# Attention stages on one Trainium2 core: turns and maxima in 64-row halves, value products in two blocks, PSUM banks in three pairs

## The chip, the cores and the metric

One core of one Trainium2 chip runs the whole program in one launch. The metric is the device time in microseconds (us). Three runs of the kernel before took 2137.2, 2140.37 and 2140.66 us; the median is 2140.37 us.

TensorE is called PE here, VectorE DVE, ScalarE ACT, GpSimd POOL, and SyncE, which issues most DMAs, SP.

## The reference, cut to what matters

Two decoder layers over x of shape (16, 256, 256), sixteen heads of 16 columns, all in fp32. Each layer is: attention over x itself, attention over a context of 77 rows, a feed-forward part. Every one of them reads its input through a layer norm and adds its output to x.

```
q, k, v = x @ Wq + bq, c @ Wk + bk, c @ Wv + bv      # c is x or the context
scores  = einsum('bhqd,bhkd->bhqk', q, k) / sqrt(16) # masked: window of 32 / causal / padding / a mask
out     = softmax(scores) @ v                        # per head
x       = x + out @ Wo + bo
```

The four attentions are of kind `window`, `cross_pad` (layer 0), `causal` and `cross_mask` (layer 1). Layer 0's feed-forward part is a mixture of eight experts, two for each row; layer 1's is a quantised gated one. The change touches neither.

## The kernel before, in words

`attention` (line 188) is called twice: for window and cross_pad, then for causal and cross_mask. Each call is one software pipeline of `N` = 32 items (a batch entry in a layer), one step an item. A step `t` works on item t (layer norm turned, q, k, v projected), item t-1 (scores, row maxima), item t-2 (scores again, shifted by the maxima, then exp and the value product) and item t-3 (last value product, heads turned and divided, output projection); item t-4's output is added to x. Every step has 8 slots, `i` = 0 to 7 (`PAIRS_H`), one for each pair of heads. Each engine runs its own written-out order of a step and meets the others only at semaphores, so the order inside `step` of each engine sets everything.

What a slot holds on PE (`step`, line 1672): `scores` (line 1536) writes the raw scores of a pair into the bank pair `ps1`, once DVE has taken the last pair's maxima (`s1_max`). `shifted` (line 1564) writes minus the row maximum (a product with `selects`) and the scores again into the bank pair `ps2`, once ACT's exp of the last pair is done (`expd`). Both take 64 rows of PE, the two halves side by side. Both bank pairs have one buffer. In the two cross layers a slot of even `i` does two pairs and a slot of odd `i` none (`L.pairs` = 2; `wide(ref)` says so of item t-2). Behind `shifted` comes what is left of the step, one thing or two a slot:

- slot 0: `turn_normed` (four 128-row transposes of the normalised x), the fourth value product `pv` of item t-3
- slot 1: the query projection, `max_out` of the second half of item t-2's maxima
- slot 2: the key projection (self-attention only), parts of the routing or of the last layer norm's turn
- slot 3: `pv` of quad 0 (a quad is four heads; 32 columns of PE each); slot 4: the value projection, `max_out` of item t-1's first half; slots 5 to 7: `pv` of quads 1 and 2, and for item t-3 the turn of the heads (line 1791), the turn of the divided output (1805) and the output projection (1819)

PSUM has four bank pairs: ps1, ps2, `pso` (value products of four quads) and `misc`, which in turn holds the turned x, q, k, v, the maxima, the heads and the output product; PE's waits on `oT_ev`, `m_ev`, `added`, `v_ev` guard it. `prob` holds two quads. DVE (line 1188) does in each slot `row_max` (line 1015), and between them: `split_max` ahead of slot 0 and in slot 3, `add_output` in 0, the next item's statistics in 1, `low_part` of q in 2 and of k in 3, the heads' reciprocal and division ahead of row_max in slot 6, `merge_rows` (causal only) in 4 to 7, `normalise` of the next item in 7. ACT (line 1404) does the exps and copies PSUM out: xT, o_aug (all four quads at once), q and k high parts, v, maxima, oT. POOL cuts the masks out of `prob` (`cut`), SP moves q and k parts into `q_pair` and `k_pair` (`stacked`).

Of the kernel before, what the change touches and what calls it, by code (L numbers as in the profile page):

```python
# [4 lines left out]
F32 = mybir.dt.float32  # L5
# [136 lines left out]
class Route:  # L142

    def __init__(self, nc, ctx, a, room):
# [18 lines left out]
        self.got_in = ctx.enter_context(nc.semaphore("moe_got_in"))  # L163
        self.half_in = ctx.enter_context(nc.semaphore("moe_half_in"))
        self.first_rows = self.got[:, 0, 0:1, :]
        self.first_rows_in = ctx.enter_context(nc.semaphore("moe_first_rows_in"))
# [5 lines left out]
        self.first_in = ctx.enter_context(nc.semaphore("moe_first_in"))  # L172
        self.first_w = [ctx.enter_context(nc.semaphore(f"moe_first_w{i}")) for i in range(3)]
# [14 lines left out]
def attention(nc, layers_in, x_sb, q_pair, k_pair, v_aug, ident, selects, to_all, eye, parts, merge=None, tail=None, route=None,  # L188
# [8 lines left out]
    with ExitStack() as ctx:  # L197
# [8 lines left out]
        prob = sb("prob", [P, 2, 2, 2, S + P], F32)  # L206
# [6 lines left out]
        masked = sb("masked", [P, 4 * S], BF16)  # L213
# [11 lines left out]
        bv_wide = sb("bv_wide", [P, KC, P], F32)  # L225
# [7 lines left out]
        if tail or route:  # L233
            last_ln = layernorm_tiles(lambda name, shape, dt: sb(f"last_{name}", shape, dt))
            last_xn = [sb("last_xn", [P, ST, D], F32)[:]] if tail else route.rows
# [60 lines left out]
        pso = pb("pso", [P, 2, 512])  # L296
        misc = pb("misc", [P, 2, 512])
# [105 lines left out]
        bank = lambda k: misc[:, k, :]  # L403
        xT_ps = bank(0).rearrange("p (k t) -> p k t", k=KC)
        q_ps = bank(1).rearrange("p (k t) -> p k t", k=KC)
        o_heads = misc[:, :, :].rearrange("p a (h d) -> p (a h) d", d=VW)
        o_by_half = o_tok[:].rearrange("p s (q a j) d -> p a (s q) j d", a=2, j=2)
        oT_ps = misc[:, :, 0:S].rearrange("p a (n t) -> p a n t", t=64)
# [3 lines left out]
        ctx_ps = lambda n: (ps2[:, 0, :], ps2[:, 1, :], pso[:, 1, :])[n % 3].rearrange("p (k t) -> p k t", k=KC)  # L412
# [7 lines left out]
        def k_ps(par, L):  # L420
            if L.cross:
                return L.k_now[par][:]
            return bank(0)[:, 0:KC * L.nk].rearrange("p (k t) -> p k t", k=KC)

        def v_ps(L):
            return bank(1)[:, 0:L.ktiles * D].rearrange("p (k h d) -> p (k h) d", k=L.ktiles, d=HD)
# [33 lines left out]
        def turned_before(ref):  # L460

            return active(ref, 2) and active(ref, 3) and layer_at(ref, 2).pairs == 1

        def cut_early(ref):

            return turned_before(ref) and layer_at(ref, 2).kind == "causal"

# [28 lines left out]
        def turn_bank(ref, k):  # L496
# [2215 lines left out]
```

## Time and profile before

| | |
|---|---|
| median of three runs | 2140.37 us |
| span of the profiled execution | 2144.3 us |
| PE / DVE / ACT / POOL busy, share of the span | 93% / 58% / 45% / 32% |
| window stage, first to last query projection | 10.9 to 305.3 us |
| cross_pad stage, the same | 323.7 to 572.1 us |
| experts between the two calls | to about 1200 us |
| causal stage | 1206.9 to 1509.5 us |
| cross_mask stage | 1527.8 to 1766.2 us |
| quantised feed-forward part | the rest |

The profile is of one execution; the page gives no time for it but its span. The sums below are in its microseconds, which stand 3.9 us above the median. A line of a timeline merges instructions that follow one another; a matmul of fp32 operands shows as two instructions.

### The profile page before, as it was taken

How to read it: one execution, taken by the hardware profiler on the slowest of the kernel's cores; microseconds unless marked ns; L12 is line 12 of the kernel's file. 1: busy time of each engine (PE TensorE's matmuls, PEld its weight loads, DVE VectorE, ACT ScalarE, POOL GpSimd, SP SyncE). 2: the span in 40 equal slices, each digit the busy share in tenths (PEclk: the TensorE clock that was granted, in tenths of full speed). 3: DMA queues.
4: the chain of work that ended last, by engine and by line, in shares of the span. 5: the costliest groups of instructions: out<-in, count | busy, mean ns of one | idle time of the engine just before them, and what ended most of it. 6: DMA issues, size and time to landing. Idle time of an engine off the chain costs nothing. (4 is left out here: it accounts for less than half of the span.)

```text
span 2144.3 us, 51295 instructions
## 1 busy us (share of the span) xinstructions
PE 2001.3 (93%) x17274; PEld 1546.4 (72%) x17274; DVE 1247.5 (58%) x5456; ACT 963.5 (45%) x1873; POOL 689.7 (32%) x1244
## 2 busy tenths in 40 slices
PE   8999998999976999999999889999999998999889
PEld 6777776666656999999999667777766665444377
DVE  6778886666642011110115588888878876459964
ACT  3555545656622333333333355555555553357400
POOL 3666665345552000000000545554422220013400
PEclk9999999999978999999999999999999999999999
DMA  7333332333318999999997534343233331000023
GB/s 221 115 104 108 108 112 90 98 104 119 109 52 322 399 343 340 340 346 338 341 342 291 160 127 129 127 132 114 93 96 103 109 104 47 0 0 1 0 61 97
DMA packets 209540, 334.50 MB, mean 156 GB/s; under 512 B 59501, under 2 KB 193426, under 8 KB 200306
## 3 DMA queue, kind: packets, MB, share of 16 engines
q1 hardware_dynamic: 194914, 301.82, 40.8%
q0 software_dynamic: 9552, 26.10, 4.0%
q10 hardware_dynamic: 4928, 4.72, 0.6%
q8 instruction: 82, 1.34, 0.3%
q14 instruction: 64, 0.52, 0.1%
HBM read 193.74 MB, written 28.05 MB: 103 GB/s over the span
## 5 line engine op out<-in xcount | busy, mean ns | idle before, releaser
L2044 ACT ACTIVATE moe_h<-moe_h_ps,moe_weights 128x128 f32<-128x128 f32 x424 | 132.4, 363 | 256.0 <-PE moe_h_ps L2012 226.2
L1339 ACT ACTIVATE causal_prob<-causal_ps 128x768 f32<-128x768 f32 (+1 forms) x192 | 168.8, 879 | 112.9 <-PE causal_ps L1592 112.0
L2477 PE MATMUL ffn_prod_ps<-x_sb,ffn_weights 128*128 128x512 f32 x480 | 209.5, 596 | 7.0 <-ACT ffn_sig_q L2463 7.0
L2076 DVE TENSOR_TENSOR moe_y<-moe_y_ps,moe_weights 128x256 f32<-128x256 f32 x53 | 22.5, 424 | 328.2 <-PE moe_y_ps L2024 328.2
L2012 PE MATMUL moe_h_ps<-moe_h,moe_weights 128*128 128x128 f32 x1696 | 198.0, 275 | 0.0
L1955 POOL DMA_DIRECT2D moe_y_dram<-moe_y x71 | 39.4, 554 | 492.1 <-DVE moe_y L2076 492.1
L2012 PEld LDWEIGHTS moe_h_ps<-moe_h,moe_weights 128*128 128x128 f32 x1696 | 193.6, 192 | 0.1
L2477 PEld LDWEIGHTS ffn_prod_ps<-x_sb,ffn_weights 128*128 128x128 f32 x480 | 90.6, 191 | 123.6 <-issue 109.3
L1029 DVE CUSTOM_DVE_ANT_0 causal_masked<-causal_ps,causal_causal_mask 128x256 bf16<-128x256 f32 (+1 forms) x512 | 152.3, 354 | 42.5 <-PE causal_ps L1558 38.5
L1029 DVE CUSTOM_DVE_ANT_0 window_masked<-window_ps,window_window_mask 128x160 bf16<-128x160 f32 x512 | 135.5, 320 | 58.6 <-PE window_ps L1558 56.0
L1339 ACT ACTIVATE window_prob<-window_ps 128x640 f32<-128x640 f32 x128 | 89.9, 703 | 97.4 <-PE window_ps L1592 96.5
L823 POOL TENSOR_SCALAR_AFFINE_SELECT causal_prob<-causal_prob 128x512 f32<-128x512 f32 x128 | 85.2, 690 | 115.5 <-ACT causal_prob L1339 115.3
L1558 PEld LDWEIGHTS causal_ps<-k_pair,q_pair 64*128 64x128 f32 x1024 | 71.9, 185 | 64.9 <-issue 33.5
L1558 PE MATMUL window_ps<-k_pair,q_pair 64*128 64x160 f32 (+1 forms) x1024 | 99.8, 296 | 16.3 <-DVE window_m_tok L1029 16.2
L2332 DVE TENSOR_REDUCE ffn_peak<-ffn_wide 128x1 f32<-128x1024 f32 x72 | 87.0, 1210 | 48.0 <-ACT ffn_wide L2437 48.0
L1558 PE MATMUL causal_ps<-k_pair,q_pair 64*128 64x78 f32 (+2 forms) x1024 | 98.0, 292 | 16.0 <-DVE causal_m_tok L1029 14.5
L1558 PEld LDWEIGHTS window_ps<-k_pair,q_pair 64*128 64x128 f32 x1024 | 74.5, 188 | 50.0 <-DVE window_m_tok L1029 28.0
L810 POOL TENSOR_SCALAR_AFFINE_SELECT window_prob<-window_prob 128x384 f32<-128x384 f32 (+1 forms) x128 | 74.5, 605 | 95.2 <-ACT window_prob L1339 95.1
L1994 PE MATMUL moe_h_ps<-moe_rowsT,moe_weights 128*128 128x128 f32 x848 | 103.5, 275 | 1.0 <-DMA moe_weights<-moe_w_in 1.0
L1029 DVE CUSTOM_DVE_ANT_0 causal_masked<-causal_ps,causal_cross_mask 128x77 bf16<-128x77 f32 x512 | 86.3, 235 | 28.4 <-PE causal_ps L1558 27.9
L2024 PE MATMUL moe_y_ps<-moe_weights,moe_h 128*128 128x256 f32 x424 | 100.4, 380 | 0.7 <-ACT moe_h L2044 0.7
L1994 PEld LDWEIGHTS moe_h_ps<-moe_rowsT,moe_weights 128*128 128x128 f32 x848 | 98.9, 192 | 1.2 <-DMA moe_weights<-moe_w_in 1.2
(404 smaller groups left out, 4699.0 us busy)
## 6 DMA issues: line engine op xcount, KB each, us to landing
moe_weights<-moe_w_in SPq DMA_DIRECT2D x53, 2180.0 KB, 9.1
q_pair<-parts SPq DMA_DIRECT2D x512, 128.0 KB
parts<-moe_w_in SPq DMA_DIRECT2D x17, 2180.0 KB
k_pair<-parts SPq DMA_DIRECT2D x256, 128.0 KB
k_pair<-parts SPq DMA_DIRECT2D x256, 38.5 KB
moe_y_dram<-moe_y POOLq DMA_DIRECT2D x71, 128.0 KB, 3.4
moe_rows<-moe_slots_dram SPq DMA_DIRECT2D x53, 128.0 KB, 3.0
x_before_ffn_dram<-x_sb SPq DMA_DIRECT2D x16, 256.0 KB, 2.1
```

What stands on the lines that cost most here:

```text
L810: op = nc.gpsimd.affine_select(out=m, in_=m, compare_op=ALU.is_ge, fill=0.0, base=base, pattern=[[0, 4], [1, width]], channel_multiplier=-1)
L823: op = nc.gpsimd.affine_select(out=m, in_=m, compare_op=ALU.is_ge, fill=0.0, base=0, pattern=[[0, 4], [1, P]], channel_multiplier=-1)
L1029: op = nc.vector.tensor_tensor_reduce(masked[:, junk * width:junk * width + nk_real], ps1[:, ab, p * L.width1 + col:p * L.width1 + col + n ...
L1339: nc.scalar.activation(out, src, ACT.Exp).then_inc(expd, 1)
L1558: op = nc.tensor.matmul(ps1[:, ab, j * L.width1 + col:j * L.width1 + col + nk], q_pair[par][rows_of[ab], i + j, qt * P:qt * P + P], k_pair ...
L1955: pool.dma_start(route.y_dram[bass.ds(j * TM, TM), :].rearrange("(s p) d -> p s d", p=P), y[r][:])\
L1994: op = nc.tensor.matmul(h1_ps[:, f // 2, (f % 2) * TM:(f % 2) * TM + TM], w1[:, k, f * P:f * P + P], rowsT[:, k, :], start=(k == 0), stop= ...
L2012: op = nc.tensor.matmul(h2_ps[:, f // 2, (f % 2) * TM:(f % 2) * TM + TM], w2[:, k, f * P:f * P + P], h1[:, k, :], start=(k == 0), stop=(k ...
L2024: op = nc.tensor.matmul(y_ps[:, r % YR, s * D:s * D + D], h2[:, k, s * P:s * P + P], w3[:, k, :], start=(k == 0), stop=(k == FB - 1))
L2044: nc.scalar.activation(out[:, f, :], psum[:, f // 2, (f % 2) * TM:(f % 2) * TM + TM], ACT.Gelu, bias=bias[:, f:f + 1]).then_inc(done, 1)
L2332: return nc.vector.tensor_reduce(out, rows, AX.XY, ALU.max, apply_absolute_value=True)
L2477: op = nc.tensor.matmul(prod_ps[:, slot, f, :].rearrange("p (b t) -> p b t", b=2), w[:, k, at:at + P], x_cols(n // GROUPS, k), start=(k == ...
```

## The change

The bank pairs are `ps1`, `ps2`, `psa` and `psb`. psa holds the value products (its first bank, two quads at a time), turned x, k, the maxima and the routing products; psb holds q, v, heads, turned output and the output product. `prob` holds all four quads, so exp doesn't wait for the quad two before it. All turns are made in 64-row halves (`turn_halves`), eight transposes of 64 columns where there were four of 128; `max_out` makes four where there were two. The value products run as two blocks of two quads: `first_quads` at the end of slot 7 (item t-2), `last_quads` in slot 1 of the next step (slot 2 in a wide step); ACT copies the heads out in two halves, `keep_heads`. The four projections are made between `scores` and `shifted` of a slot rather than behind `shifted`: output in slot 1 (now of item t-4), query 3, key 4, value 5; their waits stand a slot or half a slot ahead (phase 0). On DVE `row_max` comes first in every slot, `add_output` moves to slot 1, `low_part` of q to slot 3 behind `split_max`, of k to slot 4. `gate(pe, pe_passed)` is a semaphore increment that carries some of these waits. Semaphores are allocated differently, `bv_wide` lies in `prob`, `masked` is smaller, and the ring for POOL's DMA descriptors is set to 8192.

The core of the diff (PE's step, the new functions, DVE's order):

```diff
+                def first_quads(t, ref):
+                    wait(pe, v_ev, upto(t, ref, 0))
+                    wait(pe, m_ev, upto(t, ref, 1, 2) - 1 if active(ref, 1) else 2 * N)
+                    for qd in range(2):
+                        pv(t, ref, 2, qd)
+                def last_quads(t, ref):
+                    wait(pe, xT_ev, upto(t, ref, 0))
+                    pe.wait_ge(o_ev, (t - 3) * 2 + 1)
+                    for qd in range(2, NQ):
+                        pv(t, ref, 3, qd)
+                def turn_halves(out, rows):
+                    for k in range(KC):
                         for s in range(ST):
-                            op = nc.tensor.transpose(xT_ps[:, k, s * P:s * P + P], xn[par][:, s, k * P:k * P + P], ident[:])
+                            for ab in range(2):
+                                op = nc.tensor.transpose(out[:, ab, k * ST + s], rows[rows_of[ab], s, k * P:k * P + P],
+                                                         ident[rows_of[ab], rows_of[ab]])
+                def early_maxima(t, ref):
+                    wait(pe, k_lo, upto(t, ref, 0))
+                    wait(pe, m_ev, upto(t, ref, 2, 2))
+                    if in_tail(ref, 5):
+                        pe.wait_ge(last_ev, tail_item(t, 5) + 1)
+                    max_out(t, 1, 0)
+                def late_maxima(t, ref):
+                    wait(pe, xT_ev, upto(t, ref, 0))
+                    wait(pe, o_ev, upto(t, ref, 3, 2))
+                    max_out(t, 2, 1)
...
                     for i in range(PAIRS_H):
                         if active(ref, 1):
                             scores(t, ref, i)
+                        if i == 0 and now and narrow:
                             turn_normed(t, ref)
+                        if i == 0 and active(ref, 4) and not narrow:
+                            output(t, ref, 0)
+                        if i == 1 and active(ref, 4):
+                            output(t, ref, 1)
+                        if i == 2 and now and not narrow:
+                            query(t, ref, 0)
+                        if i == 3 and active(ref, 2):
+                            late_maxima(t, ref)
+                        if i == 3 and now:
+                            query(t, ref, 1)
+                        if i == 4 and now and not L.cross:
+                            key(t, ref, 1)
+                        if i == 4 and in_tail(ref, 5):
+                            last_turn(t, ref)
+                        if i == 5 and active(ref, 1) and not narrow:
+                            early_maxima(t, ref)
+                        if i == 5 and now:
+                            value(t, ref, 1)
+                        if i == 6 and active(ref, 3):
+                            heads_out(t, ref)
                         if active(ref, 2):
                             shifted(t, ref, i)
...
+                        if i == (1 if narrow else 2) and active(ref, 3):
+                            last_quads(t, ref)
...
+                        if i == 6 and active(ref, 1) and narrow:
+                            early_maxima(t, ref)
+                        if i == 7 and active(ref, 2):
+                            first_quads(t, ref)
                         if i == 7 and active(ref, 3):
+                            turn_outputs(t, ref)
```

```diff
                     for i in range(PAIRS_H):                      # DVE
+                        if active(ref, 1):
+                            row_max(t, ref, i)
                         if i == 6 and active(ref, 3):
                             dve.wait_ge(o_mm, t - 2)
...
+                        if i == 1 and active(ref, 4):
                             add_output(t, ref, 4)
...
-                        if i == 2 and active(ref, 0):
-                            low_part(q_parts[par], q_ps, layer_at(ref).bq, q_hi, q_lo, t, S)
...
+                        if i == 3 and active(ref, 1):
+                            split_max(t, ref, 1, 0)
                         if i == 3 and active(ref, 0):
+                            low_part(q_parts[par], q_ps, layer_at(ref).bq, q_hi, q_lo, t, S)
+                        if i == 4 and active(ref, 0):
                             L = layer_at(ref)
                             low_part(k_parts[par], k_ps(par, L), L.bk, k_hi, k_lo, t, L.nk)
```

## Rows read from the trace of the kernel before

**Rows 1.** Busy time by stretch; the columns are named in the first line.
```profile
core 0: us, PE busy (x) PEld busy (x) DVE busy (x) ACT busy (x) POOL busy (x), PEclk, DMA share, GB/s
11.00:305.00 294.00, 277.20 (x2844) 212.51 (x2845) 228.27 (x1233) 144.12 (x259) 165.74 (x298) 0.99 0.40 129
1207.00:1508.00 301.00, 283.37 (x2833) 214.89 (x2834) 253.20 (x1288) 160.63 (x285) 150.29 (x223) 0.99 0.43 133
1528.00:1766.00 238.00, 227.46 (x2465) 160.04 (x2466) 188.79 (x1375) 134.62 (x242) 67.99 (x146) 1.00 0.33 100
```

**Rows 2.** Query projection: duration ns min/median/max, first to last start, form.
```profile
L1716 PE MATMUL window_misc<-window_xT,first_wq x128: 379/379/792, 10.9 to 305.3; 128*128 128x256 f32 x128
L1716 PE MATMUL window_misc<-window_xT,window_cross_pad_wq x128: 379/379/484, 323.7 to 572.1; 128*128 128x256 f32 x128
L1716 PE MATMUL causal_misc<-causal_xT,first_wq x128: 379/379/483, 1206.9 to 1509.5; 128*128 128x256 f32 x128
L1716 PE MATMUL causal_misc<-causal_xT,causal_cross_mask_wq x128: 379/379/484, 1527.8 to 1766.2; 128*128 128x256 f32 x128
```

**Rows 3.** Timeline of PE, window stage: start us, us, operation, [idle before <-releaser].
```profile
156.66 0.71 PE L1791 MATMUL window_misc<-ident,window_o_aug 64*128 64x64 f32 x16
157.30 0.75 PE L1614 MATMUL window_pso<-window_prob,v_aug 128*32 128x160 f32 x16
...
159.75 0.45 PE L1558 MATMUL window_ps<-k_pair,q_pair 64*128 64x160 f32 x4 [0.56 <-DVE window_m_tok L1029]
...
160.50 0.75 PE L1614 MATMUL window_pso<-window_prob,v_aug 128*32 128x160 f32 x16
161.18 1.99 PE L1819 MATMUL window_misc<-window_window_wo,window_oT 128*128 128x256 f32 x8
163.11 0.45 PE L1558 MATMUL window_ps<-k_pair,q_pair 64*128 64x160 f32 x4
...
163.86 0.66 PE L1663 MATMUL window_misc<-ident,window_xn 128*128 128x128 f32 x4
164.45 0.75 PE L1614 MATMUL window_pso<-window_prob,v_aug 128*32 128x160 f32 x16
```

**Rows 4.** Timeline of DVE, the same step.
```profile
157.43 0.35 DVE L1200 RECIPROCAL window_recip<-window_misc 128x32 f32<-128x32 f32 x1
...
158.62 0.32 DVE L1029 CUSTOM_DVE_ANT_0 window_masked<-window_ps,window_window_mask 128x160 bf16<-128x160 f32 x1
...
160.40 0.32 DVE L1029 CUSTOM_DVE_ANT_0 window_masked<-window_ps,window_window_mask 128x160 bf16<-128x160 f32 x1 [0.70 <-PE window_ps L1558]
...
161.38 0.94 DVE L87 TENSOR_SCALAR window_xn<-x_sb,window_mv,window_rstd 128x256 f32 x2
162.24 0.67 DVE L1007 CAST window_m_cols<-window_m_tok 128x8 fp32r<-128x8 f32 x2
...
163.76 0.32 DVE L1029 CUSTOM_DVE_ANT_0 window_masked<-window_ps,window_window_mask 128x160 bf16<-128x160 f32 x1
```

**Rows 5.** Timeline of PE, cross_mask stage.
```profile
1640.93 1.99 PE L1716 MATMUL causal_misc<-causal_xT,causal_cross_mask_wq 128*128 128x256 f32 x8
1642.76 0.38 PE L1669 MATMUL causal_misc<-ident,causal_m_cols 128*85 128x128 f32 x2
1643.08 0.64 PE L1558 MATMUL causal_ps<-k_pair,q_pair 64*128 64x78 f32 x8
...
1644.33 0.44 PE L1626 MATMUL causal_misc<-ident,causal_last_xn 128*128 128x128 f32 x2
```

**Rows 6.** Timeline of ACT, the same stretch.
```profile
1641.49 1.01 ACT L1437 ACTIVATE causal_o_aug<-causal_pso 128x1024 f32<-128x1024 f32 x1
...
1643.46 0.82 ACT L1307 ACTIVATE parts<-causal_misc,causal_cross_mask_bq 128x256 fp32r<-128x256 f32 x2
```

**Rows 7.** Timeline of DVE, the same stretch.
```profile
1643.91 0.24 DVE L1029 CUSTOM_DVE_ANT_0 causal_masked<-causal_ps,causal_cross_mask 128x77 bf16<-128x77 f32 x1 [1.45 <-PE causal_ps L1558]
...
1645.18 0.87 DVE L993 SCALAR_TENSOR_TENSOR parts<-causal_misc,causal_cross_mask_bq,parts 128x256 fp32r<-128x256 f32 x2
...
1647.02 0.48 DVE L993 SCALAR_TENSOR_TENSOR parts<-causal_cross_mask_k_now,causal_cross_mask_bk,parts 128x77 fp32r<-128x77 f32 x2
```

More of the change, by code:

```diff
@@ L494, in emptied, with bias_slot @@
             return bool(tail) and ref >= N + 2
-        def turn_bank(ref, k):
-            return ps1[:, k, 0:S] if emptied(ref) else bank(0)[:, S:2 * S]
+        def bias_slot(ref):
+            return 2 if ref else 5
         def tail_item(t, lag):
@@ L1471, in step @@
+                    if ahead(ref, 6) or ahead(ref, 7):
+                        see(t + 1, ref + 1)
                     if ref == 0:
@@ new lines, in whole, with query @@
+                def whole(out, lhs, rhs):
+                    for f in range(2):
+                        for k in range(KC):
+                            op = nc.tensor.matmul(out(f), lhs(f, k), rhs(f, k), start=(k == 0), stop=(k == KC - 1))
+                    return op
+                def query(t, ref, phase):
+                    L = layer_at(ref)
+                    of = (lambda f: q_ps[:, f, :], lambda f, k: L.wq[:, k, f * P:f * P + P], lambda f, k: xT[:, k, :])
+                    if phase == 0:
+                        pe.wait_ge(xT_ev, t + 1)
+                        wait(pe, added, upto(t, ref, 4))
+                        wait(pe, q_lo, upto(t, ref, 1))
+                        if ref >= 2:
+                            pe.wait_ge(v_ev, t)
+                        if active(ref, 4):
+                            pe.wait_ge(oT_ev, t - 3)
+                        gate(pe, pe_passed)
+                    if phase:
+                        whole(*of).then_inc(q_mm, 1)
@@ new lines, in output, with heads_out @@
+                def output(t, ref, phase):
+                    O = layer_at(ref, 4)
+                    of = (lambda f: psb[:, f, 0:D], lambda f, k: oT[:, k, f * P:f * P + P], lambda f, k: O.wo[:, k, :])
+                    if phase == 0:
+                        pe.wait_ge(oT_ev, t - 3)
+                    if phase:
+                        whole(*of).then_inc(proj_mm, 1)
+                def heads_out(t, ref):
+                    pe.wait_ge(o_ev, (t - 3) * 2 + 2)
+                    wait(pe, v_ev, upto(t, ref, 0))
+                    wait(pe, added, upto(t, ref, 4))
+                    gate(pe, pe_passed)
+                    for s in range(ST):
+                        for q in range(4):
+                            first = (s * 4 + q) * 64
+                            for ab in range(2):
+                                op = nc.tensor.transpose(psb[:, ab, first:first + 64], o_aug[rows_of[ab], q, s * P:s * P + P],
+                                                         ident[rows_of[ab], rows_of[ab]])
+                    op.then_inc(o_mm, 1)
@@ L1837, in _ @@
                     pe.wait_ge(added, N)
-                    nc.tensor.matmul(bank(1)[:, 0:NE], route.ones[:], route.filled[:], start=True, stop=True).then_inc(total_mm, 1)
+                    nc.tensor.matmul(psb[:, 0, 0:NE], route.ones[:], route.filled[:], start=True, stop=True).then_inc(total_mm, 1)
                     pe.wait_ge(gate_exp, 1)
```

501 lines of the change are left out of this document (234 added, 267 removed).

## The prediction, made before the changed kernel had run

> **What bounds the kernel now.** I read the busy shares of the four attention stretches first, then the spacing of the query projections, then PE and DVE beside each other through one step. PE is busy 277.2 of 294.0 us in the window stretch, 283.4 of 301 in causal, 227.5 of 238 in cross_mask: 94 to 96%, at a granted clock of 0.99 to 1.00, so 2.4 GHz [rows 1]. A step is (305.3 - 10.9 - 1.8) / 15 = 19.5 us in window, 16.4 in cross_pad, 20.1 in causal, 15.8 in cross_mask (some 15.5 in its middle) [rows 2]; 16 steps of each are 1150 us, and the change touches nothing else. So PE bounds, but only just: in window DVE is busy 228.3 of 294, 15.1 us of each 19.5, in causal 253.2 of 301, 16.9 of 20.1 [rows 1]. And the two are tied: ps1 has one buffer, so scores of slot i+1 wait for the maxima of slot i. Scores start at 159.75, the maxima at 160.40 (0.65 later) and take 161.38 - 160.40 = 0.98; the ones before started at 158.62, so ended at 159.60, and PE went on at 159.75 (0.15) after 0.56 idle [rows 3, 4]. A narrow slot can't be shorter than 0.65 + 0.98 + 0.15 = 1.78 us. PE's own load of a slot is 0.75 (scores to the end of shifted, 160.50 - 159.75) plus what is put into it. The step is short now because the other work is spread such that nearly every slot's load is over 1.78, and because the longest piece, the output projection (1.93, 163.11 - 161.18), stands in slot 7, where DVE has most to do behind its maxima [rows 3, 4].
>
> **PE's work, part by part** (window). Turned x: 0.59 now (164.45 - 163.86). The sixteen half turns of the heads take 157.30 - 156.66 = 0.64, 0.04 each; eight are 0.32: -0.27. Two maxima turns: 0.32 each now (1643.08 - 1642.76), 0.16 in halves: -0.32 [rows 3, 5]. Bounds for both: nothing saved, or all but the 0.04 of one turn. Value products: 0.68 each alone (161.18 - 160.50) [rows 3]; a quad that follows another has no entry to pay. Its price isn't in the trace; it lies between 0.68 and its share without entry, and I take 0.57: a block is 1.25, -0.22 a step. The projections are 1.93 between 64-row neighbours, and 1.83 where a turn of the maxima in 128 rows follows (1642.76 - 1640.93) [rows 3, 5]; now all have 64-row neighbours: +0.2 for two. The sum is -0.6 of 18.4 us, 17.8.
>
> The pages bear on this twice. Where a block of other row shape comes in or goes out, the rows show some 0.1 us (1.93 against 1.83). The Trainium skill (TensorEngine Tiling (Array Packing), Key Properties) says that a change of tiling mode drains the engine; with seven whole-array blocks a step before and six after it speaks for the change, by the row's 0.1 an end with 0.2 us a step, which my sum has in other terms. Against it speaks the same page's Instruction Overhead: about 60 cycles with each matmul, whatever its width. By that eight turns of 64 columns would take 8 x 124 / 2.4 GHz = 0.41 us, an estimate from the page, and the x turn would save 0.18 rather than 0.27. The trace's 0.04 a turn is less than its 0.052.
>
> **What the new order does to the narrow steps.** Take slots 6, 7 and 0 together. DVE must do, in a row: maxima 6, the reciprocal and division (157.43 to 158.62: 1.19; they now stand behind maxima 6), maxima 7, the next item's normalisation (0.86), the split of the maxima (162.24 to 163.76: 1.52), maxima 0 [rows 4]. From scores 6 to scores 1 that is 0.65 + 0.98 + 1.19 + 0.98 + 0.86 + 1.52 + 0.98 + 0.15 = 7.3 us. PE holds for it three groups of 0.75, heads 0.64, maxima 0.16, two quads 1.25, two turns 0.64: 4.9. Before, the same stretch also had the output projection, two more quads, and its x turn was longer, and PE filled it. Now 2.4 us are idle: first at the x turn, which waits for the normalisation (`normed`), then at scores 1. Slot 2 has nothing on PE but its group, as `query`'s phase 0 is only waits: 1.78, of which 1.0 idle. Slot 1 has 0.75 + 1.93 + 1.25 = 3.9, with DVE waiting for the projection; what DVE loses there it can't get back. Slot 3: 0.75 + 0.16 + 1.93 = 2.8; slots 4 and 5: 2.7 each. In 3 to 5 the query's way over ACT (0.82) and DVE (0.87) to maxima 4 is about as long as PE's work beside it [rows 6, 7]; I charge nothing, and if that cover is gone it is 0.2 to 0.4 a step. Sum: 7.3 + 3.9 + 1.8 + 2.8 + 2.7 + 2.7 = 21.2 against 19.5. The split of 1.52 is the dearest reading (POOL works beside it), so I take +1.5 a step: 24 us in 16. Bounds: -0.6 a step, if no new wait came, to +2.
>
> Causal has the same order; DVE has 1.8 us more a step [rows 1], the merges in slots 4 to 7 above all, half of it in the stretch from 6 to 0. That stretch becomes 8.2, slot 2 1.9, and the value products are wider than window's both before and after: about 22.2 against 20.1, +2.1, 34 us. Exp no longer waits for a quad's buffer in prob, but it isn't what is late in either.
>
> **The wide steps.** Here scores and shifted come in even slots only, and DVE has room. New is a chain within a step: the query product ends 1.83 after its start; ACT's high part 0.82; DVE's low part 0.87; maxima 4, eight operations from 1643.91 to 1645.18, 1.27, now ahead of k's low part, 0.48 [rows 5 to 7]. Only then may PE turn the early maxima (`k_lo` in `early_maxima`), and the value product, heads and slot 6 are queued behind. With 0.4 for three hand-overs that is 5.7 us after the query's start; PE has the product 1.83, the group of slot 4 (1644.33 - 1643.08 = 1.25) and the last norm's turn 0.3, 3.4 in all [rows 5]. Idle: 2.1 with the group's ends counted. Second, psa's bank is now shared: `late_maxima` waits for ACT's copy of the two quads before it (half of 1.01 [rows 6], and two hand-overs: 0.8), with slot 3 having no scores to hide it. Third, smaller: heads to turned output over DVE with maxima 6 ahead (0.6), copied oT ahead of shifted 0 (0.4), `added` ahead of slot 2's shifted (0.4). Together 4.3 us of waits. PE's work falls from 14.8 (96% of 15.5) by 1.0: turns 0.3, maxima 0.3, last turn 0.3, quads 0.3, less 0.2 for ends. 13.8 + 4.3 = 18.1 against 15.5: +2.6, of which I take 2.5: 40 us. Bounds: -1.0, if all is hidden, to +3.3. In cross_pad maxima are one reduction, half as long, and the routing products stand between the quads and the late maxima in 10 of 16 steps: idle 1.5 + 0.3, and PE's saving 0.8: +0.8, 13 us.
>
> SP issues the q parts a slot later, with two slots and more left before scores 0; POOL's copy into v_aug waits for the last quads, so until slot 1 or 2 of the next step, with its cuts behind it; there are 2 to 3 us of room in window. Neither is on the path. Smaller DMA rings cost nothing unless the four gathers of a step fill one.
>
> Sum: 24 + 34 + 40 + 13 = 111, less some 6 for the first and last steps of both calls, which lack part of the waits: +105 on the profiled 2144.3, so 2249; on the median of 2140.4 it is **2245 us**, 5% slower.
>
> **The rivals.** (a) PE stays the bound and its savings count: DVE has 3 to 4 us of slack a step [rows 1], and the chains may run beside other work better than I see. Saved are 0.6 (window), 0.7 (causal), 1.0, 0.8 a step: 16 x 3.1 = 50 us, 2090. Against it: slot 2 and the stretch from 7 to 1 hold too little PE work for DVE's orders, whatever PE costs. It decides if the idle time added is under 0.8 us a step. (b) A draw: narrow steps slower by half my figure, wide ones faster by theirs; 2140. It needs `k_lo` to be early, which the order of DVE forbids. (c) More waits than found: the cover in slots 3 to 5 is gone (0.4 in 32 steps, 13 us), POOL's late copy delays the context for k in cross_pad (1 us in 16 steps), each `gate` keeps PE from loading ahead (0.1 for six of them, 38 us in 64 steps): 67 us on top, 2310. For it: before each group PE loads early; nothing shows the price.
>
> **How the numbers follow.** My forecast 0.72, with 2205 to 2280 as its own range; (a) 0.12, (b) 0.05, (c) 0.11. 0.2% either way is what a measurement here can tell from nothing. Faster: (a), 0.12; same: 0.03 of (b); slower: the rest, 0.85. The range of 2155 to 2295 leaves out (a) and the far end of (c).
>
> **What would show it.** Query projections 21 us apart in window, 22.2 in causal, 18 in cross_mask, 17.2 in cross_pad; PE busy 85% in window and 77% in cross_mask, at the same clock; PE idle before scores 1 and scores 3 with DVE's maxima as releaser, before the x turn with the normalisation, before the early maxima of wide steps with k's low part. Eight x turns in 0.3 us and a block of two quads in 1.25 show the savings. I am wrong if the spacing in window stays under 19.5, or if the wide steps' idle time before the early maxima is under 1 us.

## The result, and the profile after

The changed kernel takes 2364.35 us (median of 4 runs, 2358.85 to 2368.8) against 2139.14 for the kernel before beside it: 1.1049 times as long, 95% interval 1.1027 to 1.107. The forecast was 2245, at most 2295. The sign was right; the 105 us forecast are less than half of the 225 that came. The profiled execution has a span of 2357.2 us against 2144.3, 212.9 more.

First the granted clock of the two, before and then after (span, mean clock of the core).

```profile
core 0: 2144.3 us, clock 0.981
```

```profile
core 0: 2357.2 us, clock 0.937
```

Now busy time from the first query projection of each stretch to its sixteenth (window, cross_pad, causal, cross_mask); columns as in [rows 1], with PEclk third from the end. First the kernel before, in these windows:

```profile
10.90:303.71 292.81, 276.01 (x2839) 211.46 (x2839) 226.98 (x1224) 143.12 (x258) 165.50 (x297) 0.99 0.40 129
323.74:570.48 246.74, 227.06 (x2573) 163.40 (x2571) 156.34 (x593) 147.96 (x269) 118.02 (x272) 1.00 0.34 103
1206.92:1507.84 300.92, 283.29 (x2833) 214.81 (x2833) 253.04 (x1288) 160.47 (x285) 150.28 (x224) 0.99 0.43 134
1527.83:1764.57 236.74, 226.20 (x2463) 158.93 (x2459) 188.69 (x1375) 133.37 (x241) 67.01 (x143) 1.00 0.33 100
```

The changed kernel:

```profile
11.00:339.98 328.98, 288.39 (x2970) 221.35 (x2971) 227.97 (x1243) 148.82 (x273) 164.75 (x300) 0.94 0.36 115
361.01:669.72 308.71, 254.17 (x2811) 195.96 (x2807) 167.05 (x582) 153.38 (x274) 118.45 (x274) 0.88 0.27 82
1297.68:1648.98 351.30, 301.12 (x2965) 229.19 (x2965) 262.10 (x1307) 164.98 (x300) 149.31 (x226) 0.93 0.37 115
1670.63:1972.28 301.65, 243.89 (x2685) 182.67 (x2683) 199.82 (x1377) 140.96 (x245) 66.04 (x142) 0.91 0.26 79
```

The four sum to 1290.64 us against 1077.21: 213.4 more, all of the difference. PE is busy longer (1087.6 against 1012.6 us) although its work is a little less (0.1 to 0.3 us a step, below), because part of it runs at 1.2 GHz. 2 x (1 - PEclk) x length gives the time at that level; read from the clock's records without rounding it is 37.5, 75.1, 47.8 and 54.6 us, 215.0 in all, where the kernel before had 5.8, 0, 3.4 and 0. In the whole span it is 299.9 us against 85.0.

What a microsecond at 1.2 GHz costs shows in two successive window steps of the changed kernel, query to query:

```profile
210.45:231.47 21.02, 18.65 (x219) 14.73 (x216) 15.75 (x86) 10.49 (x19) 11.85 (x22) 1.00 0.30 100
231.47:254.14 22.67, 20.18 (x219) 15.62 (x216) 15.78 (x86) 10.40 (x19) 11.78 (x22) 0.92 0.28 93
```

The same 219 matmuls, 1.65 us more for 3.4 us at half clock: 0.48 us each. By that price (215.0 - 9.2) x 0.48 = 99 of the 213.4 us go with the clock. The remaining 114.6 are 21, 26, 29 and 39 us by stretch; for the same 15 steps the prediction had 22.5, 12, 31.5 and 37.5, 103.5 in all. The division is an estimate, and 99 its upper end, since a microsecond of waiting can hide one at half clock. Two successive steps of cross_mask show it, the first at full clock throughout:

```profile
1788.44:1807.70 19.26, 14.73 (x178) 10.94 (x177) 13.38 (x95) 9.33 (x16) 3.71 (x9) 1.00 0.28 86
1807.70:1829.14 21.44, 17.41 (x178) 12.92 (x176) 13.29 (x94) 9.23 (x16) 4.40 (x11) 0.84 0.25 76
```

Here 6.8 us at half clock cost 2.18 us, 0.32 each. e5 tests the division.

The first of the two window steps on PE (start us, us, [idle before <-releaser]) answers to [rows 3]:

```profile
218.54 0.71 PE L1836 MATMUL window_psb<-ident,window_o_aug 64*128 64x64 f32 x16
219.13 0.41 PE L1633 MATMUL window_ps<-window_m_rows,selects 64*128 64x320 f32 x2
...
221.06 1.29 PE L1658 MATMUL window_psa<-window_prob,v_aug 128*32 128x160 f32 x32
222.29 0.46 PE L1729 MATMUL window_psb<-ident,window_o_tok 64*128 64x64 f32 x8
222.56 0.43 PE L1604 MATMUL window_ps<-k_pair,q_pair 64*128 64x160 f32 x4
223.16 0.46 PE L1729 MATMUL window_psa<-ident,window_xn 64*128 64x64 f32 x8 [0.18 <-ACT window_o_aug L1405]
223.46 0.42 PE L1633 MATMUL window_ps<-window_m_rows,selects 64*128 64x320 f32 x2
...
225.06 0.45 PE L1604 MATMUL window_ps<-k_pair,q_pair 64*128 64x160 f32 x4 [1.00 <-DVE window_m_tok L1026]
225.44 1.99 PE L1771 MATMUL window_psb<-window_window_wo,window_oT 128*128 128x256 f32 x8
...
230.90 0.45 PE L1604 MATMUL window_ps<-k_pair,q_pair 64*128 64x160 f32 x4 [0.95 <-DVE window_m_tok L1026]
```

The forecast savings of these parts are there: eight x turns in 0.30 (223.46 - 223.16), two quads in 1.23. So are the idle places before scores 1 (1.00) and scores 3 (0.95). In the next step the output projection right behind the first of them runs at 1.2 GHz and takes 3.46 us:

```profile
246.12 0.45 PE L1604 MATMUL window_ps<-k_pair,q_pair 64*128 64x160 f32 x4 [0.93 <-DVE window_m_tok L1026]
246.50 3.46 PE L1771 MATMUL window_psb<-window_window_wo,window_oT 128*128 128x256 f32 x8
```

The Trainium skill (TensorE: Matmul & The Clock Gate, A second HAM failure mode: psum-queue depth-cycling) tells of a measured kernel in which PE idles briefly but often between groups of matmuls, swings between its two clock levels and loses throughput by it. The trace agrees: with two idle places of some 1 us a step, every third or fourth window step behind the third has 3.4 us at 1.2 GHz.

A cross_mask step, which answers to [rows 5, 7]:

```profile
1807.41 0.36 PE L1747 MATMUL causal_psa<-ident,causal_m_cols 64*85 64x64 f32 x4 [1.01 <-ACT causal_o_aug L1405]
1807.70 1.99 PE L1771 MATMUL causal_psb<-causal_xT,causal_cross_mask_wq 128*128 128x256 f32 x8
...
1813.48 0.48 PE L1747 MATMUL causal_psa<-ident,causal_m_cols 64*85 64x64 f32 x4 [2.25 <-DVE parts L990]
1813.89 1.99 PE L1771 MATMUL causal_psb<-causal_cross_mask_wv,causal_cross_mask_ctx_b 128*77 128x128 f32 x8
```

The waits are 1.01 us before the late maxima and 2.25 before the early ones (forecast 0.8 and 2.1), as they are in the step at full clock before it; the value product behind the second takes 1.99 us at 1.2 GHz; at 2.4 it is 1.07 (in e8, below).

### The profile page after: what moved, and what is told of

Its sections match the earlier page's. It is cut to its first block and busy times, and to the rows that moved or that the text cites. A ratio compares the mean times of both kernels' runs of the same rounds, so it can differ in the third digit from the quotient of the medians.

```text
span 2357.2 us, 53374 instructions
## 1 busy us (share of the span) xinstructions
PE 2070.7 (88%) x18042; PEld 1628.8 (69%) x18042; DVE 1275.7 (54%) x5456; ACT 984.3 (42%) x1905; POOL 685.7 (29%) x1244
## 5 line engine op out<-in xcount | busy, mean ns | idle before, releaser
L2179 DVE TENSOR_TENSOR moe_y<-moe_y_ps,moe_weights 128x256 f32<-128x256 f32 x53 | 22.5, 425 | 328.1 <-PE moe_y_ps L2127 328.1
L2058 POOL DMA_DIRECT2D moe_y_dram<-moe_y x71 | 39.5, 557 | 491.9 <-DVE moe_y L2179 483.7
L1604 PEld LDWEIGHTS causal_ps<-k_pair,q_pair 64*128 64x128 f32 x1024 | 77.4, 199 | 68.0 <-DVE causal_m_tok L1026 41.1
L894 POOL COPY v_aug<-causal_v_stage 128x512 f32<-128x512 f32 (+1 forms) x32 | 16.1, 503 | 356.1 <-PE causal_psa L1658 289.0
L1604 PEld LDWEIGHTS window_ps<-k_pair,q_pair 64*128 64x128 f32 x1024 | 80.4, 203 | 48.4 <-DVE window_m_tok L1026 35.7
L1331 ACT ACTIVATE window_prob<-window_ps,window_padT 77x1024 f32<-77x1024 f32 x64 | 71.1, 1111 | 89.0 <-PE window_ps L1638 89.0
L2097 PE MATMUL moe_h_ps<-moe_rowsT,moe_weights 128*128 128x128 f32 x848 | 103.5, 275 | 1.0 <-DMA moe_weights<-moe_w_in 1.0
```

What stands on the lines that cost most here:

```text
L1331: nc.scalar.activation(out, src, ACT.Exp, bias=pad).then_inc(expd, 1)
L1604: op = nc.tensor.matmul(ps1[:, ab, j * L.width1 + col:j * L.width1 + col + nk], q_pair[par][rows_of[ab], i + j, qt * P:qt * P + P], k_pair ...
L2097: op = nc.tensor.matmul(h1_ps[:, f // 2, (f % 2) * TM:(f % 2) * TM + TM], w1[:, k, f * P:f * P + P], rowsT[:, k, :], start=(k == 0), stop= ...
```

## The experiments

Times are medians, with the kernel before at 2138 to 2141 us in each comparison. Stretches are from first to sixteenth query projection, in us; the last column is their time at 1.2 GHz. They are of one profiled execution of each kernel, which took up to 14 us more (e7) or 9 us less (e10) than the median, so differences of stretches and of times don't agree exactly. The edits shown are shortened.

| run | time | ratio, 95% interval | window | cross_pad | causal | cross_mask | 1.2 GHz |
|---|---|---|---|---|---|---|---|
| before | 2139.1 | | 292.8 | 246.7 | 300.9 | 236.7 | 9 |
| after | 2364.4 | 1.1027 to 1.107 | 329.0 | 308.7 | 351.3 | 301.6 | 215 |
| e1 | 2369.6 | 1.1039 to 1.1098 | 333.2 | 301.9 | 352.3 | 306.0 | 64 |
| e2 | 2329.7 | 1.084 to 1.0906 | 314.5 | 310.5 | 328.8 | 306.0 | 191 |
| e3 | 2367.6 | 1.1021 to 1.1109 | 329.0 | 318.4 | 352.1 | 294.6 | 215 |
| e4 | 2401.3 | 1.1152 to 1.1265 | 325.8 | 326.2 | 349.9 | 322.7 | 272 |
| e5 | 2325.6 | 1.0854 to 1.0898 | 320.3 | 302.3 | 340.1 | 292.1 | 85 |
| e6 | 2302.4 | 1.0745 to 1.0781 | 297.0 | 309.5 | 324.5 | 307.5 | 177 |
| e7 | 2347.3 | 1.0965 to 1.1002 | 328.7 | 312.4 | 352.4 | 287.0 | 211 |
| e8 | 2284.6 | 1.0624 to 1.0729 | 296.1 | 307.3 | 323.8 | 282.7 | 126 |
| e9 | 2257.0 | 1.052 to 1.0577 | 297.0 | 300.7 | 323.1 | 272.1 | 123 |
| e10 | 2217.5 | 1.0347 to 1.041 | 302.0 | 260.6 | 321.7 | 259.9 | 65 |
| e11 | 2402.3 | 1.1207 to 1.1268 | 328.1 | 341.1 | 352.3 | 307.2 | 249 |
| e12 | 2216.1 | 1.0342 to 1.0393 | 295.1 | 263.2 | 322.8 | 263.9 | 61 |
| e13 | 2337.5 | 1.0907 to 1.0957 | 326.9 | 291.5 | 352.4 | 294.6 | 201 |
| e14 | 2157.7 | 1.0071 to 1.0117 | 298.2 | 244.0 | 311.0 | 237.1 | 19 |

**e1 and e5: PE kept at work in its idle places.**

```diff
+def fill(n):
+    for _ in range(n):
+        nc.tensor.matmul(psb[:, 0, S:S + P], ident[:], ident[:], start=True, stop=True)
+if i == 0 and now and active(ref, 4) and narrow: fill(6)      # e5: 3; the same at i == 2
+if i == 3 and now and active(ref, 4) and not narrow: fill(5)  # e5: 3; ahead of late_maxima
+if i == 5 and now and active(ref, 4) and not narrow: fill(12 if tail else 7)  # e5: 8, 4; early_maxima
```

> Dummy matmuls of 128 columns into an unused bank stand where PE is idle in the changed kernel: six at the end of slots 0 and 2 of narrow steps, five ahead of the late maxima and seven (second call: twelve) ahead of the early maxima of wide steps. The output is untouched and no wait is removed. Theory A (the waits cost the 110 us forecast, and PE's idle places are also followed by stretches at 1.2 GHz, 205 us more of them than before, which cost the other 100): most of the half-clock stretches go, the spacing of the queries in a window step stays at 21.0 us, and the time falls by 60 to 100 us, to 2265 to 2305. Theory B (the further loss is more waits, of which the granted clock is only a mark): nothing falls, and what the dummies hold up of PE adds 5 to 30 us, 2370 to 2395.

> As e1_fill, with fewer dummies: one took 0.27 us there, so six were 1.6 us in an idle place of 1.0. Now three stand at the end of slots 0 and 2 of narrow steps (0.8 us), three ahead of the late maxima and four (second call: eight) ahead of the early maxima of wide steps. No wait is removed. Theory A (what a half-clock stretch costs is a loss of its own, on top of the waits): steps keep the full-clock spacing of the changed kernel (21.0 in window, 22.4 in causal, about 18.3 in cross_mask) and hardly any half-clock stretch is left, so 2364 falls by 60 to 90 us, to 2275 to 2305. Theory B (the granted clock only marks waits, and filling them gives nothing): 2355 to 2375.

e1: 64 us at 1.2 GHz instead of 215, yet no gain; taken alone, its 2369.6 us are what theory B said to within a microsecond (2370 to 2395). But the dummies were too long:

```profile
210.37 1.60 PE L1851 MATMUL window_psb<-ident 128*128 128x128 f32 x12
```

Six (12 matmul records) take 1.60 us in an idle place of 1.0, so a window step is 22.0 us, where it was 21.0 at full clock. That is why e1 can't decide. e5 has fewer of them: behind the third, window steps are 20.9 to 21.1 us without exception, and its first and last stretch show

```profile
10.99:331.28 320.29, 299.42 (x3115) 233.40 (x3115) 227.63 (x1243) 148.88 (x273) 163.77 (x300) 0.97 0.36 118
1650.47:1942.54 292.07, 262.35 (x2989) 203.84 (x2987) 199.75 (x1377) 141.69 (x245) 65.97 (x142) 0.99 0.27 82
```

39 us less than the changed kernel with no wait removed, between the two theories' ranges (2275 to 2305 and 2355 to 2375): B, by which nothing falls, is out. Behind the third narrow step no time at 1.2 GHz is left, though the order of PE's products and its waits are unchanged: the idle places are what the clock fell behind. But 130 us less at 1.2 GHz should give 62 by the price above. The narrow stretches gained 20 us for 48 us less at 1.2 GHz, 0.42 each; the wide ones 16 us for 82, 0.2 each. How much of the rest the dummies take back themselves (in cross_pad PE waits for the stacks 19.6 us instead of 12.1), and how much time at 1.2 GHz lay beside waits anyway, isn't separated; cross_mask steps took 19.1 to 19.5 us at full clock, the changed kernel's 19.26. So some 39 us of the loss are the clock's own, and 99 is the upper end of the estimate.

**e2 and e6: PE work for the narrow idle places.** e2:

```diff
+if i == 0 and active(ref, 4) and narrow:      # behind scores 0, ahead of turn_normed
+    output(t, ref, 0); output(t, ref, 1)
+if i == 7 and active(ref, 3) and narrow:      # ahead of first_quads; ACT: keep_oT ahead of keep_heads
+    turn_outputs(t, ref)
```

> Narrow steps only: the output projection stands between the scores and the turned x of slot 0 (and its turns ahead of the two quads of slot 7, ACT's copy of oT ahead of the heads' copies), so that 1.9 us of PE's work lie beside DVE's normalisation and split of maxima. My account of the narrow step (slots 6, 7 and 0 hold 7.3 us of DVE's chain against 4.9 us of PE's) says 21.0 -> 19.3 us, 1.7 us in some 28 steps = 48 us, and a higher mean granted clock in window and causal with 10 to 30 us more: 2285 to 2315. If the loss of narrow steps lies elsewhere (in the blocks of two quads or the gates), the projection only moves its place: within 10 us of 2364.

35 us less, where I expected 49 to 79. A window step went to 20.35 us, not 19.3: shifted 0 now ran behind the projection, so its exponential came late and PE waited 0.67 us before shifted 1. Behind the third, its narrow steps had no time at 1.2 GHz, though that place and the one of 0.95 us before scores 3 stood in each. e6 puts half a product behind shifted instead:

```diff
 def query(t, ref, phase):                     # output likewise
     if phase == 0:
...
+        if not wide(ref): whole(*of, fs=(0,))
     if phase:
-        whole(*of).then_inc(q_mm, 1)
+        whole(*of, fs=(0, 1) if wide(ref) else (1,)).then_inc(q_mm, 1)
```

> Narrow steps only: the first half (f = 0) of the query's and of the output's products stands where only their waits stood (end of slots 2 and 0), the second half where the whole stood. Each half is 0.97 us and falls into an idle place of 0.95 to 1.0 us (before scores 3 and scores 1). If these two places are the loss of the narrow steps as I put it, a step goes from 21.0 to 19.2 us in window and from 22.4 to 20.7 in causal, 28 steps x 1.8 = 50 us, with 25 to 45 us more from the granted clock: 2270 to 2290. If the narrow slots are bound by something else (DVE's orders all along, blocks whose rows change more often), under 15 us.

```profile
205.74 1.13 PE L1771 MATMUL window_psb<-window_window_wo,window_oT 128*128 128x256 f32 x4
206.86 0.45 PE L1604 MATMUL window_ps<-k_pair,q_pair 64*128 64x160 f32 x4
...
210.82 1.13 PE L1771 MATMUL window_psb<-window_xT,first_wq 128*128 128x256 f32 x4
211.88 0.45 PE L1604 MATMUL window_ps<-k_pair,q_pair 64*128 64x160 f32 x4
```

Both idle places are gone. A window step is 19.4 us (19.6 before the change), a causal one 21.85 where I expected 20.7; there DVE is busy 263 of 324 us, and PE still waits 0.9 a step for the normalisation (11.6 us in 13 times). Behind the third step no narrow step has any time at 1.2 GHz. 62 us less (expected 74 to 94).

**e3, e4, e7, e9: the wide steps.**

```diff
-if i == 4 and active(ref, 0):                                  # e3, DVE
+if active(ref, 0) and i == (3 if layer_at(ref).cross else 4):
     low_part(k_parts...)
```

> Cross layers only: DVE writes k's low part in its slot 3, ahead of maxima 4, and not behind it. My account of the wide step (early maxima wait for maxima 4 and then for k's low part) says that the idle time of 2.25 us before the early maxima falls by about 1.3 in cross_mask and 0.7 in cross_pad: 21 + 11 = 32 us, and 10 to 40 us more if the granted clock rises with it: 2290 to 2325. If PE's waits there end elsewhere (the query's low part, or the half-clock stretches come whatever the wait), at most 10 us.

The wait before the early maxima fell as expected (24.2 to 11.8 us in the first call, 30.0 to 14.4 in the second); cross_mask gained 7 us, cross_pad lost 10, and in all nothing was gained. Waits of PE in e3 (us in total, times, longest):

```profile
PE window_ps L1597 <- DMA k_pair<-parts: 31.8, 14, 3.3
PE causal_psa L1747 <- DVE parts L990: 14.4, 14, 1.2
PE causal_ps L1604 <- DMA k_pair<-parts: 12.6, 14, 1.7
```

In the changed kernel the first is 12.1. The first scores wait for the stack of k: the next limit. e4 moves the late maxima instead; ACT writes their rows right behind exp 2, and the quads wait for that.

```diff
+if i == 2 and not narrow: maxima_first(t, ref)    # max_out(t, 2, 1) ahead of last_quads
```

> Wide steps only: the late maxima stand in slot 2 ahead of the last two quads and not in slot 3 behind them, so that they wait for no copy of the quads. The idle time of 1.0 us before them goes: 1.0 x 32 steps = 32 us at most, less what other waits take back: 2330 to 2350 by my account, lower if the granted clock rises with it. If the bank's hand-over is hidden by what follows anyway, no change.

37 us slower. The wait for ACT's copy went, but the quads, now behind the maxima in psa, waited 44.3 us for ACT's rows of them; 57 us more at 1.2 GHz. A miss. e7 lets PE do its products first:

```diff
+if i == 3 and now and not narrow: query(t, ref, 1)    # ahead of late_maxima
+if i == 5 and now: value(t, ref, 1)                   # ahead of early_maxima
```

> Wide steps only: in slot 3 the query product stands ahead of the late maxima, and in slot 5 the value product ahead of the early maxima. So PE has 1.9 and 1.1 us of work where it waited 1.0 us for ACT's copy and 2.25 us for k's low part, and the query's chain begins 1.3 us earlier. My account says 1.0 + 2.0 us less a step in cross_mask and 0.9 + 1.2 in cross_pad: about 75 us less at the same clock, and more if the granted clock rises: 2265 to 2300. Rival: the stack of q and k for the next step, or the exponential after the late maxima, is then late, and takes half of it back: 2310 to 2335.

> e6_split and e7_products_first together. Theory A (waits as forecast, and the clock on top): the two add up, 2170 to 2210. Rival: they don't, since the loss stands elsewhere: 2300 or more.

e7 gained 17 us and e8 80: e6 and e7 add up (62 + 17), but e7 falls short of its 64 to 99 (and of its rival's 29 to 54), and e8 with it of 2210, without reaching its rival's 2300. A cross_mask step at full clock became 17.7, not 15.3. e8 shows why:

```profile
1770.20 1.99 PE L1771 MATMUL causal_psb<-causal_xT,causal_cross_mask_wq 128*128 128x256 f32 x8
...
1775.28 1.07 PE L1771 MATMUL causal_psb<-causal_cross_mask_wv,causal_cross_mask_ctx_b 128*77 128x128 f32 x8 [1.02 <-DVE parts L990]
1776.96 0.36 PE L1747 MATMUL causal_psa<-ident,causal_m_cols 64*85 64x64 f32 x4 [0.61 <-DVE parts L990]
...
1781.64 0.64 PE L1604 MATMUL causal_ps<-k_pair,q_pair 64*128 64x78 f32 x8 [0.68 <-DMA k_pair<-parts]
```

The query product ends at 1772.1, but ACT first writes the rows of the maxima and k's high part, so q's low part is ready only at 1775, and the value product, which shares psb with q, waits for it. e9 reorders these two engines and puts the value product back behind the early maxima:

```diff
+if now and layer_at(ref).cross:               # ACT, ahead of max_rows(t, ref, 2, 1)
+    key_high(t, ref); query_high(t, ref)
+if i == 3 and active(ref, 0) and L.cross:     # DVE, ahead of q's low part
+    low_part(k_parts...)
```

> e6_split for the narrow steps; wide steps: the query product stands ahead of the late maxima, ACT writes k's high part in slot 2 and q's high part ahead of the rows of the maxima, and DVE writes k's low part ahead of q's low part, so before maxima 4. The value product stays behind the early maxima. My account (the early maxima are late only because k's low part is queued behind maxima 4, and the value product because q's low part is late) says that in cross_mask the idle places of 1.0 (late maxima) and 2.25 us (early maxima) fall to under 1 together and a step goes from 18.3 to 16.0 us: against e8_split_and_first (17.7 in cross_mask) 1.7 x 30 = 50 us less, and more with the clock: 2200 to 2240. Rival: the stack of q and k (the transfers behind the parts) is what the next step's first scores wait for, so steps stay at 17.5 or more and the time at 2270 to 2300.

28 us less than e8, between the two ranges (2200 to 2240 and 2270 to 2300); cross_mask steps 17.2, not 16.0. In part the rival holds: PE's waits for the stacks are 37 us.

**e10, e11, e13: the stacks.** SP issues 16 transfers a step; in e9 (start us, us of four issues):

```profile
1765.31 2.48 SPq L624 DMA_DIRECT2D q_pair<-parts  x4
1767.90 2.47 SPq L631 DMA_DIRECT2D k_pair<-parts  x4
1770.49 2.46 SPq L624 DMA_DIRECT2D q_pair<-parts  x4
1773.00 2.54 SPq L631 DMA_DIRECT2D k_pair<-parts  x4
```

Query product until 1762.92, stacks from 1765.31, first half issued at 1770.37, first scores at 1771.80, the next query product at 1778.31. That is a loop of its own.

```diff
+for stack in ((stack_k, stack_q) if cross else (stack_q, stack_k)):    # SP, per half
+    stack(hf, pairs)
```

> e9_chains_early, and in cross layers SP stacks k's first half ahead of q's (k's parts are ready there before q's product ends). In e9 the stacks of a step took four times 2.5 us in a row from q's low part on, and the first scores of the next step waited for the second of the four (0.6 us in cross_mask, up to 3.6 in cross_pad, 37 us in all). Theory: the loop query product -> parts -> 5 us of stacking -> first scores -> query product bounds the wide steps now that the query product stands two slots later than before the change, so stacking 2.5 us of it early takes these 37 us and some clock loss away: 2195 to 2225. Rival: the transfers are late for another reason (the whole of the two stacks is needed, or the queue is just as late), and the time stays at 2250 to 2260.

39.5 us less, as expected: cross_pad 300.7 to 260.6, and time at 1.2 GHz 123 to 65 us. Stretches of e10 (cross_pad, cross_mask):

```profile
332.40:592.98 260.58, 228.97 (x2812) 177.22 (x2811) 168.02 (x590) 150.68 (x274) 119.57 (x277) 0.97 0.32 97
1563.67:1823.60 259.93, 225.26 (x2690) 169.61 (x2686) 198.47 (x1380) 139.51 (x245) 66.54 (x143) 0.99 0.30 92
```

> The changed kernel with two edits for cross layers alone: k's low part ahead of maxima 4 (as e3_k_low_early) and SP stacking k's halves ahead of q's (as e10). PE's order is that of the changed kernel. e3 shortened the wait before the early maxima by half and gained nothing, while waits for the stacks rose from 12 to 44 us. If those stacks took the gain back, it now comes: cross_pad 318 -> about 280 us, cross_mask 295 -> about 285, the time 2310 to 2335. If e3's miss has another cause (the granted clock, or psa's bank), the time stays at 2355 to 2370.

e11 missed: 38 us slower than the changed kernel. On DVE k's low part still stood behind q's, so stacking k first only began later, and PE waited 68.8 us for the stacks (44.4 in e3). e13 is the cut that e11 should have been: all of e9's and e10's edits on ACT, DVE and SP, PE as in the changed kernel.

> The changed kernel with PE's order untouched. Cross layers only: ACT writes k's high part in slot 2 and q's ahead of the rows of the maxima, DVE writes k's low part ahead of q's low part, SP stacks k's halves ahead of q's. Theory (in the changed kernel the way from the query product over parts and stacks to the next first scores is on the path, and k's low part holds the early maxima): cross_pad 309 -> 275, cross_mask 302 -> 275, so 2300 to 2320. Rival (the chain matters only once PE's products have been moved ahead, as in e9 and e10): both within 10 us of the changed kernel, 2345 to 2365.

27 us less, between theory and rival: cross_pad 291.5 (-17), cross_mask 294.6 (-7). At full clock a cross_mask step is 17.8 to 18.1 (19.26 in the changed kernel), but from the ninth on every second one has 10.2 us at 1.2 GHz and takes 22.0 to 22.9, up to 4.7 more: 0.46 for each us, close to the window's price.

**e12 and e14.** e12: K_SLOTS = (1, 3, 5, 6), and ACT's copies with them.

> e10_k_stack_first, and in the second step of each call the third to sixth part of the context's key product stand in slots 1, 3, 5, 6 and not 3, 5, 6, 7, so that 1.6 us of PE's work fall where PE is idle three times (1.07, 1.36, 0.5 us) and runs at 1.2 GHz afterwards. If idle places lower the clock there as in the steady steps, the first three steps get 5 to 12 us shorter in each call: 2195 to 2210. If not, 2210 to 2220.

The window's first steps gained 7 us, cross_mask lost 4; 1.4 us in all is no difference, and the time stays in the second range (2210 to 2220).

```diff
+for s in range(ST):        # e14: the kernel before, DVE ahead of normalise
+    nc.vector.tensor_scalar(spare_xn[:, s, :], in_x(t + 1, ref + 1)(t + 1, s)[:, 0:224], ...)
```

> The kernel before the change, with DVE's normalisation of the next item preceded by two operations of 224 columns into a spare tile (0.9 us a step, at the place where the changed kernel's narrow steps lose theirs). If PE's idle places lower the granted clock whatever the order: window 292.8 -> 310 to 320 us, of it 13 the added wait and the rest half-clock stretches (10 us of them or more in window and causal, where there were 9); 2175 to 2195 in all. If the clock falls only with the new order: no new half-clock stretches, 2145 to 2170.

Window steps went from 19.65 to 19.87 only, causal ones from 20.35 to 20.97: DVE had the room (in the window step from 203 us on PE's idle places are 0.15 to 0.59), and the clock stayed at 2.4 GHz in the steady steps. Only the first steps took more time at 1.2 GHz (19 us against 9 in all). 2157.7 us lie in the range of the second theory, that the clock falls only with the new order, but no idle place came near 1 us here, so the run doesn't tell the two apart.

## Why the prediction was wrong

- **The step that failed: "PE busy 85% in window and 77% in cross_mask, at the same clock".** The sum priced each wait at its length, with PE's work at 2.4 GHz as in [rows 1]. The waits came, and with them 206 us more at 1.2 GHz (busy shares of 88% and 81% over the stretches, 89% and 76% in the steps at full clock). The price is 99 us by the pair of window steps, some 60 if a microsecond costs 0.2 in the wide stretches, as in e5; e5 bought 39 back with dummies alone, and e6 and e10, which took idle places away, lost time at 1.2 GHz with them (215 to 177, 123 to 65). No rival priced it, so the range missed it as well.
- **"Neither is on the path", of SP's stacks: wrong in the wide steps.** The query product moved two slots nearer to the first scores that need its stack. PE waited 12.1 us for it in the changed kernel's cross_pad (up to 3.2 at a time). In e3 that rose to 31.8 there and 12.6 in cross_mask, 32 us more, where the maxima's waits fell by 28. The early and late maxima cost cross_pad more than forecast too (1.7 and 0.6 us a step, not 1.5 and 0.3). With PE's order mended the stacks were worth 39.5 us (e10 against e9). In the unmended one the whole chain was worth 27 (e13), not separated further.
- **PE's work: the parts came, the saving of 0.6 and 1.0 us a step didn't.** x turn 0.59 to 0.30, two quads 1.23 against 1.25; the maxima take 0.23 to 0.30, not 0.16. But a steady step of the kernel before holds this (window, then cross_mask, in columns as above):

```profile
165.89:185.58 19.69, 18.73 (x211) 14.60 (x209) 15.88 (x87) 10.21 (x19) 11.97 (x22) 1.00 0.32 107
1625.49:1640.93 15.44, 15.01 (x164) 10.40 (x160) 12.66 (x93) 8.74 (x17) 4.07 (x9) 1.00 0.36 107
```

  PE is busy 18.65 us in the changed kernel's window step at full clock (18.73 before) and 14.73 in cross_mask's (15.01): 0.1 and 0.3 less. One reason is a term that the sum left at nothing: projections now stand between a slot's scores and its shifted, and these two came to more. Their part alone (tiles window_ps) of the window step, before and after:

```profile
165.89:185.58 19.69, 6.60 (x82) 5.35 (x80) 8.45 (x33) 5.63 (x8) 1.00 0.32 107
210.45:231.47 21.02, 7.48 (x80) 5.66 (x80) 8.42 (x32) 5.63 (x8) 1.00 0.30 100
```

  In cross_mask it is 5.49 to 6.04 us (tiles causal_ps). The other is the start of the sum, 18.4 us of work in window, a mean that takes in the stage's first steps, which hold fewer matmuls. The second weighing from the Trainium skill (TensorEngine Tiling (Array Packing), Instruction Overhead) would have had the eight turns at 0.41 by adding 60 cycles to each turn's 64 (the section can also be read as a least time for each); the trace has 0.30.
- **Narrow steps: right in time, in part by luck.** 21.0 us in window (forecast 21.0), 22.4 in causal (22.2), idle before scores 1 and 3 as said; before the x turn with the normalisation in causal (0.9 us), but only 0.18 and with ACT in window. A window step is 18.65 us of work and 2.4 idle, where the sum's parts were 17.8 and 3.4: two errors that nearly cancel. e6 removed both places and 1.6 us a window step. Causal's gain was 0.55 of the 1.7 expected: DVE stands close behind there.
- **cross_mask: the waits right, the step not.** Idle 2.25 and 1.01 at the places named, 4.5 in the steady step at full clock (forecast 4.3); but that step takes 19.26 us, not 18.1, since PE's work in it is 14.7 and not 13.8. Freeing one wait bared the next: the stacks in e3, q's low part behind ACT's order in e8, the stacks again in e9.
- **A slip in cross_pad's sum.** Its own terms, 1.5 + 0.3 - 0.8, give 1.0 a step, not 0.8; that is 3 us in 16 steps.
- **"Less some 6 for the first and last steps": wrong sign.** The first three spacings sum to 70.1 us against 56.6 in window and 70.4 against 56.8 in causal, 13.5 more each, with 23.9 and 20.5 us of them at 1.2 GHz (5.8 and 3.4 before).
- Rivals (a) and (b) fall. (c) came nearest with 2310, but not by its terms as far as they were seen: the cover in slots 3 to 5 held in window (no idle there); gates and POOL's copy weren't tried by themselves.

No version beats the kernel before. e10 and e12 stand 77 us above it, and e10's profiled execution has 9 us of its excess in window, 14 in cross_pad, 21 in causal, 23 in cross_mask, with 56 us more at 1.2 GHz in the four.

## What to carry to other kernels

Ask of each new wait what PE's clock does behind it: where PE was busy 95% and is to be 85%, price part of its work at the lower level, and look at the granted clock before anything else in the result. Small idle places are filled better by cutting a product in two (e6, 62 us in the narrow steps alone) than by dummies (e5, 39 us in all), and dummies help only while they are shorter than the place (e1 gained nothing). Count PE's work in a steady step, and add what a product costs that is put between two short groups. Where a product is moved later in a step, follow its result to the next step (parts, transfers, first scores): that loop has a length of its own, and it decides once the first waits are gone.

## What the runs showed that I had not expected

- The same busy share of PE, another clock: e10's cross_mask stretch has PE busy 225.26 of 259.93 us (87%) at a clock of 0.99, the changed kernel's window 288.39 of 328.98 (88%) at 0.94. e10's cross_mask steps have several idle places of 0.3 to 0.7 us, the window steps two of 0.95 to 1.0 within 6 us; e2's window steps, with one of 0.67 and one of 0.95, kept the full clock behind the third step. How the idle time is laid out goes with the clock; what exactly the chip looks for wasn't measured.
- An issue of SP for a stack takes 0.62 us (2.48 for four), so 16 of them fill 10 of the 17 us of a wide step.
- Dummies of 128 columns in fp32 take 0.27 us each, two matmul records apiece.
